# Repricing a planner: TensorE's chain products and the spreads are booked longer, and seven ranks differ

## The reference, cut to what matters

```python
x = x + L0_attn(layernorm(x))           # phase 0: 16 heads, causal linear attention
x = x + L0_xattn(layernorm(x), ctx)     # phase 1: 16 heads, softmax over 512 keys with a mask
x = x + L0_ffn(layernorm(x))            # 8 experts, the best 2 of them gated
x = x + L1_attn(layernorm(x))           # phase 2: 16 heads, softmax in a causal window
x = x + L1_xattn(layernorm(x), ctx)     # phase 3: 8 heads, softmax over 512 keys, then a feed-forward
x = x + L1_ffn(x)                       # ternary weights, gelu
```

## Time and profile before

| | us |
|---|---|
| median of 3 runs | 895.78 |
| lowest, highest | 891.18, 896.17 |
| profiled execution, its own time | 894.7 |
| its span (first to last instruction) | 892.9 |
| TensorE busy in the span | 776.4 |
| mean granted TensorE clock, share of full | 0.941 |

### The profile page before, as it was taken

How to read it: one execution, slowest core, us unless ns; L and a number is a source line. 1 busy time by engine, 2 the same in 40 slices (tenths; PEclk the granted TensorE clock), 3 DMA queues, 4 the chain that set the end, 5 groups by cost and what they waited for, 6 DMA issues and landing times.

```text
span 892.9 us, 18862 instructions
## 1 busy us (share of the span) xinstructions
PE 776.4 (87%) x6106; PEld 421.5 (47%) x6106; DVE 656.8 (74%) x2253; ACT 479.7 (54%) x998; POOL 356.8 (40%) x904
## 2 busy tenths in 40 slices
PE   1688599999999888978899999999999988968865
PEld 0346334443445545546465544555544544543444
DVE  6568767878888876867788888987898867557331
ACT  3423256564656456656556665467655754834623
POOL 8875102121234443445465322245333434443134
PEclk9779799999999899999999999999999998988967
DMA  9698903011304465534827422144325153054000
GB/s 297 142 184 202 167 9 58 9 51 33 80 21 102 104 137 107 114 59 81 182 67 137 102 51 56 38 101 95 82 59 98 48 112 78 12 120 69 2 0 12
DMA packets 123810, 77.70 MB, mean 87 GB/s; under 512 B 8184, under 2 KB 122048, under 8 KB 123584
## 3 DMA queue, kind: packets, MB, share of 16 engines
q1 hardware_dynamic: 123712, 76.50, 39.9%
HBM read 41.90 MB, written 32.90 MB: 84 GB/s over the span
## 4 chain that ended last, share of the span: by engine, by line
PE 60%; DVE 14%; DMA 7%; issue 6%; ACT 5%; POOL 5%; SPq 3%; DVEq 0%; POOLq 0%; ACTq 0%
PE ob L1297 10%; PE mb L1245 8%; PE eb L1273 5%; PE eb L1274 5%; PE side L1165 3%; PE side L1156 3%; PE side L1173 3%; DMA QP<-bounce 2%; PE eb L1277 2%; PE eb L1268 2%; DMA QW<-bounce 2%; PE side L1092 2%; PE eb L1270 2%; ACT probs L1481 2%; DVE junk L1758 2%
## 5 line engine op out<-in xcount | busy, mean ns | idle before, releaser
L1481 ACT ACTIVATE probs<-eb 128x512 f32<-128x512 f32 (+1 forms) x512 | 274.3, 568 | 197.4 <-PE eb L1274 103.4
L1758 DVE CUSTOM_DVE_ANT_0 junk<-mb,maskq_add 128x512 bf16<-128x512 f32 x256 | 169.5, 689 | 41.2 <-PE mb L1245 36.2
L1297 PE MATMUL ob<-probs,V 128*32 128x256 f32 (+1 forms) x2048 | 130.4, 372 | 2.2 <-ACT probs L1481 2.1
L1063 POOL TENSOR_SCALAR nm<-mx 128x8 bf16<-128x8 f32 x80 | 19.9, 248 | 238.5 <-DVE mx L1758 132.8
L1273 PE MATMUL eb<-maskk_add,identb 128*128 128x512 bf16 x256 | 98.1, 383 | 7.8 <-issue 6.4
L1766 DVE TENSOR_REDUCE mx<-mb 128x1 f32<-128x512 f32 x128 | 83.4, 686 | 28.1 <-PE mb L1245 26.6
L1245 PE MATMUL mb<-KS,QP 128*128 128x512 bf16 x256 | 91.1, 391 | 9.6 <-DVE mx L1758 6.3
L1274 PE MATMUL eb<-QP,KS 128*128 128x512 bf16 x256 | 97.8, 382 | 0.0
L967 POOL TENSOR_SCALAR rstd<-mv 128x2 f32<-128x2 f32 x64 | 16.6, 259 | 178.1 <-DVE mv L1544 176.9
L1297 PEld LDWEIGHTS ob<-probs,V 128*32 128x32 f32 x2048 | 54.6, 109 | 59.5 <-issue 30.4
L1245 PE MATMUL mb<-KS,QW 112*128 112x512 bf16 x128 | 49.3, 420 | 12.4 <-DVE mx L1766 8.0
(11 more groups left out here) (196 smaller groups left out, 1592.7 us busy)
## 6 DMA issues: line engine op xcount, KB each, us to landing
QP<-bounce SPq DMA_DIRECT2D x48, 256.0 KB, 5.6
KS<-bounce SPq DMA_DIRECT2D x32, 384.0 KB, 7.0
bounce<-scratch SPq DMA_DIRECT2D x48, 192.0 KB, 2.3
bounce<-scratch SPq DMA_DIRECT2D x64, 128.0 KB, 2.1
KS<-bounce SPq DMA_DIRECT2D x32, 192.0 KB, 4.2
bounce<-scratch SPq DMA_DIRECT2D x16, 384.0 KB, 2.6
bounce<-scratch SPq DMA_DIRECT2D x16, 256.0 KB, 3.0
bounce<-scratch SPq DMA_DIRECT2D x48, 64.0 KB, 1.8
```

Source lines behind the costliest of these rows:

```text
L1297: ins = nc.tensor.matmul(bank[32 * j:32 * j + 32, S - n:S], v_of(core, kt, 4 * g + j), pr[:, (j % 2) * n:(j % 2 + 1) * n], start=(first_ a ...
L1481: nc.scalar.activation(probs[:, u % PROBS, 0:n], eb[:, u % 2, 0:n], ACT.Exp, scale=SCALE[core.p]).then_inc(probs_by[1], 1)
L1758: ins = V_.tensor_tensor_reduce(junk[:, e.n % 2, :], bank, maskq_add[:, t, :], 1.0, NEG_EXP, ALU.add, ALU.max, mx[slot][:, t, h:h + 1])
```

## The change

Chain products on TensorE are booked at 1.7 times their listed duration as long as the plan's clock is below 75 us, and at 1.03 times after that. A spread is booked to land 2.3 us after its issue, before 2.0. Seven entries are added to the ranks, none is taken away: in `URGENT` the ends of batches 3 (1) and 5 (3) and the chains to0 of batches 0 (3) and 1 (-1); in `LATER` the chain to0 of batch 1 (-3); in `AFTER` the phase-3 cores of batches 0 (1) and 5 (-3). No instruction of the program is added or removed; the order on each engine is another.

```diff
 SHORT_PE, SHORT_BY = 0.38, 0.38
+COLD, COLD_PE, WARM_PE = 75.0, 1.7, 1.03
...
-ROW_SP, ROW_LANDS, SPREAD_LANDS = (0, 1.65, 1.65, 2.82), 2.0, 2.0
+ROW_SP, ROW_LANDS, SPREAD_LANDS = (0, 1.65, 1.65, 2.82), 2.0, 2.3
...
-URGENT = {("end", 2): 1, ("end", 4): 2, ("to0", 3): 3, ("to1", 1): 3, ("to1", 6): 1, ("to1", 7): -1, ("to3", 5): 3}
-LATER = {("end", 2): 2, ("end", 4): 3, ("end", 5): 3, ("to0", 3): 2, ("to0", 6): -2, ("to0", 7): 2, ("to1", 1): 2, ("to1", 5): 1, ("to1", 7): -3}
-AFTER = {(2, 0): -1, (2, 4): 2, (2, 7): -2, (3, 2): 3, (3, 7): 1}
+URGENT = {("end", 2): 1, ("end", 3): 1, ("end", 4): 2, ("end", 5): 3, ("to0", 0): 3, ("to0", 1): -1, ("to0", 3): 3, ("to1", 1): 3, ("to1", 6): 1,
+    ("to1", 7): -1, ("to3", 5): 3}
+LATER = {("end", 2): 2, ("end", 4): 3, ("end", 5): 3, ("to0", 1): -3, ("to0", 3): 2, ("to0", 6): -2, ("to0", 7): 2, ("to1", 1): 2, ("to1", 5): 1,
+    ("to1", 7): -3}
+AFTER = {(2, 0): -1, (2, 4): 2, (2, 7): -2, (3, 0): 1, (3, 2): 3, (3, 5): -3, (3, 7): 1}
...
             if kind == "chain":
                 _, name, us, _ = what
+                us *= 1.0 if e != "pe" else COLD_PE if t < COLD else WARM_PE
                 at_step[e][run.lane] += 1
```

## The result

The changed kernel takes 900.60 us (median of 20 runs, 894.61 to 909.28), the kernel before in the same runs 894.56 (887.37 to 901.03): a ratio of 1.0065, with a 95% interval from 1.0046 to 1.0084. It is 6.0 us slower, where 885 was forecast; 900.6 lies in the range, and on the other side of the kernel before. The profiled execution took 901.81 us (span 900.0, clock 0.947); its counterpart before 894.7 (span 892.9).

A forecast was written before the change was run, and what follows sets the result against it. Bound: TensorE's work plus places at the start, middle and near the end where a chain of few batches gates everything. 2.5 + 8.3 = 10.8 us off 894.7 gives 883.9, 885 for the median; range 871 to 908.

The forecast's parts named there:

- the cost of the prices: Whole kernel: prices add no instruction and cost nothing at run time; the 1.03, 8.0 us in the plan's books, counts nothing.
- the full stages: 112.2 to 300 and 480 to 720 us: TensorE has next to no room, so an order can give nothing.
- The 1.7: First 75 us: right from 20 to 50, too much from 50 on; effect between 0 and 6.2 us, taken at zero.
- The spreads: Waits for stacked queries, 5.1 us together: booking spreads at 2.3 us wins half, 2.5 us.
- Batch 1 first: Start, 86.0 to 112.2 us: a wider stagger of the first phase-1 cores, +10.5 to -10.5 us, taken at zero.
- the two bounds that I set for the start: First exp unit of phase 1: before 105 us means the much faster case, after 118 the start's loss.
- the much faster rival: Start, 86.0 to 112.2 us: its 10.5 us idle go beside the 10.8; 874.5 us median, chance 0.11.
- The ends of 3 and 5: 720 to 817.8 us: the last two phase-3 chains no longer stand behind an end, so 8.3 us of waits go.
- The two AFTER entries: (3, 0) delayed mid-kernel: nothing, limit 22.9 us both ways; (3, 5) preferred for maxima, counted with the ends' 8.3 us.
- The ends did not pile up: Rival, after the last exp unit: a third end lies there, up to 14.0 us more, about 909 us; chance 0.24.
- the waits only move: Rival, whole kernel: each stall that goes comes back one core later; 890 to 899 us, put at 894; chance 0.32.
- The last sentence of the prediction: Middle, 300 to 480 us: prediction wrong above all if reshuffled by more than the 22.9 us idle there suggest.

The follow-up runs named there:

- e1: The changed kernel's new prices with the ranks of the kernel before: 911.32 us against 894.74, ratio 1.0179.
- e9: The kernel before with only the 1.03 price on TensorE chain products after 75 us added: 926.77 us against 895.35, ratio 1.036.
- e8: The kernel before with only the 1.7 price on TensorE chain products before 75 us added: 901.32 us against 895.35, ratio 1.006.
- e2: The kernel before, old prices, with only the two URGENT ranks for the ends of batches 3 and 5 added: 894.65 us against 894.74, ratio 0.999.
- e6: The kernel before with the exp units of core (0, 5) held until core (1, 6) has begun: 915.25 us against 894.74, ratio 1.0218.
- r_oldp13: The kernel before, old prices, with eight ranks added by a new search: 892.15 us against 892.33, ratio 1.0002.
- r_oldp11: The kernel before, old prices, with seven ranks added from another result of the search: 894.09 us against 892.33, ratio 1.0024.
- e4: The changed kernel's new ranks with the old prices: 918.62 us against 892.80 for the kernel before, ratio 1.0282.
- e3: The changed kernel without the two URGENT ranks for the ends of batches 3 and 5: 914.92 us against 894.74 for the kernel before, ratio 1.0204.
- e5: The changed kernel with the exp units of core (1, 6) held until core (0, 5) has begun: 905.70 us against 895.35 for the kernel before, ratio 1.0129.
- e7: The changed kernel with the end of batch 0 given 3 in LATER: 892.19 us against 895.35 for the kernel before, ratio 0.9965.

## Why the prediction was wrong, point by point

**The step that failed** is the cost of the prices: "I count it at nothing; both ends, a gain from fewer late steps and a loss from steps placed later than need be, are under the wait for a single product, 0.6 us", together with "There an order can give nothing, since it removes no product", said of the full stages. The prices alone cost 16.6 us (e1). The second sentence is true of gains. It is false of losses: the stage was full because the order fed it, and an order that stacks one core late leaves it waiting. The 0.6 us rested on the thought that a price moves a step by its own size. It moves choices: in the plan, to0 of batch 5 begins at 433 instead of 411 and is stacked at 470 instead of 444, the rows of (1, 6) are there at 458, so (1, 6) is begun first, and from there the cores follow in another order. On the chip the queries of (0, 5) come 13.1 us behind the last exp unit of (3, 4) instead of 6.6 ahead, and TensorE, idle for 0.6 us between the marks before, is idle for up to 9.9. The 3% on the price of a product alone cost 31.4 us (e9). The prediction read the trace and not the plan; `plan()` by itself has the late core, and an end of 867.6 against 846.3.

**The 1.7, taken at zero.** Alone it costs 6.0 us (e8). That is near the upper end of my 0 to 6.2, by luck: the loss lies behind 576 and not in the stage that is priced. The reading of the earlier trace rows was wrong as well. Of the four slow products of L1188 two started at 61.8 and 62.6 us, where I had the price as too much, and how slow these products are differs between executions of one order (last section).

**The spreads, 2.5 us.** The longer booking by itself was not run, so the 2.5 us are neither shown nor refuted. TensorE's waits for stacked queries (QP from bounce) are 5.1 us before, 3.0 in after and none in e1, but there other cores wait, and e1 is slower all the same. In the plan alone the 2.3 moves before's end from 846.3 to 870.5, so it is no small price either.

**Batch 1 first, taken at zero.** The first exp unit of phase 1 comes at 109.54, 2.7 us ahead of before, between the two bounds that I set for the start. Neither part can claim it: six profiles with the old price before 75 us and batch 0 still first (before, e2, e6, e9, and with other ranks r_oldp13, r_oldp11) have it at 112.23 to 115.86; with the new prices alone it is at 108.97 (e1), with the 1.7 alone at 108.51 (e8), with the new ranks alone at 109.05 (e4), and with both at 109.54 to 110.99 (after, e3, e5, e7). Each alone gives about 5, both together about 4. By the mark at 467 the lead has grown to 10.2 us, the size of the much faster rival, but not by its mechanism: idle time up to the mark is about the same (at most 72.1 us against 71.5), while the chains' products, 656 against 659, take 142.78 us instead of 153.44.

**The ends of 3 and 5, 8.3 us.** The size was nearly right, by luck: the cause was not. After gains 7.2 us between the last exp units of (2, 5) and (3, 7), its waits for QW are 1.21 and 1.29 instead of 2.22 and 1.41, and there is no wait like the 4.66 of the earlier trace rows there. But the two ranks alone bring nothing (e2), so they don't do it by what I named, that a chain no longer stands behind an end. They count under the new prices only, by 14.3 us (e3).

**The two AFTER entries**, bounded by 22.9 us, do nothing in after: with and without them its plan gives the same lists on every engine.

**The rivals.** The ends did not pile up: the tail after the last exp unit is 48 us as before, with 29.41 us of the chains' products against 28.03:

```profile
852.00:900.00 48.00, 29.41 (x120) 0.68 0.02 6
```

Of "the waits only move" the result is nearest to the size (900.6, where it had 890 to 899) and has not the reason: nothing came back one core later; gains of 17.8 us met a loss of 24.9, the sums of the last column by sign. The last sentence of the prediction named the middle as what would break it, with 300 to 480 as the place and its idle time as the measure. The order was indeed changed there, where to0 of batch 5 begins late, but the time was lost in the stage behind, from 467 to 579, the one that had next to no idle time; that there was none to be had was no protection.

## What to carry to other kernels

Ranks of a planned order belong to the prices with which they were searched: new prices with old ranks, or new ranks with old prices, lost 16.6 and 25.8 us here, so change a price and search again, and judge a price by the kernels that a search finds with it, not by the first time that it gives. Run the planner before predicting from a trace: it has the cores that come late. A stage without idle time tells that an order can't gain there, and nothing about what it can lose: ask by when each core must be stacked for the exp units not to wait. In a profile with a reshuffled order, hold the two kernels together at marks such as the last exp unit of a core; gains and losses that cancel in the total show there.

## What the runs showed of the hardware that was not expected

The clock of an early stage differed between executions of one and the same order. e2 and e6 keep the order of before until the middle of the kernel, and from 43 to 86 us TensorE had 0.90 and 0.98 of its clock where before had 0.87 (before, e2, e6):

```profile
43.00:86.00 43.00, 35.81 (x462) 0.87 0.91 194
...
43.00:86.00 43.00, 34.96 (x463) 0.90 0.89 196
...
43.00:86.00 43.00, 32.31 (x462) 0.98 0.90 194
```

The six 512-wide products with the context before 75 us (side<-cT,W) took 1057 ns at the median before, 624 in e2 and 594 in e6 (count, ns least/median/most, first and last start):

```profile
L1190 PE MATMUL side<-cT,W x6: 592/624/1061, 47.2 to 70.9; 128*128 128x512 f32 x6
...
L1190 PE MATMUL side<-cT,W x6: 592/594/652, 47.0 to 69.2; 128*128 128x512 f32 x6
```

After has 0.95 and 594 ns, which is within what the old order gives, so no run shows that the new order raised the clock. The price of 1.7 was read from one execution; another of the same order shows next to none of it in these products.

Where an order left TensorE gaps, it lost its clock in the middle of the kernel too: 0.71 and 0.66 in e6 where before has 1.00. In steps of 2 us, TensorE is busy for 3.60 of the 6 us from 590 to 596, the clock falls to 0.50, the level of 1.2 GHz, and rises again behind 600, with TensorE busy throughout from 596:

```profile
592.00:594.00 2.00, 1.00 (x5) 1.00 0.57 200
594.00:596.00 2.00, 1.30 (x5) 0.57 0.03 6
596.00:598.00 2.00, 2.00 (x10) 0.50 0.00 0
600.00:602.00 2.00, 2.00 (x11) 0.72 0.00 0
```

By the Trainium skill, "TensorE: Matmul & The Clock Gate", Part 1, activity releases the throttled state; the traces agree here, with these numbers. A swap in the order so costs twice, by the gaps and by the products beside them.
